# Last even unit of a two-layer cross-attention kernel: V's third block in another gap, and its neighbours in another sequence

## What is computed

```python
def layer(x, ctx, Wq, Wk, Wv, Wo, bias):
    q, k, v = heads(x @ Wq), heads(ctx @ Wk), heads(ctx @ Wv)
    p = softmax(q @ k.T / sqrt(16))
    return merge(p @ v) @ Wo + bias + x
out = layer(layer(x, ctx, *L0), ctx, *L1)
```

## Time and profile before

| what | value |
|---|---|
| device time, median of 3 runs | 936.1 us (931.59, 936.1, 936.99) |
| profiled execution, device time | 934.22 us |
| its span | 932.4 us |
| PE busy | 902.8 us, 97% |
| DVE, ACT, POOL busy | 683.0, 543.1, 399.8 us |

### The profile page before, as it was taken

How to read it: one execution, slowest core, us unless ns; L and a number is a source line. 1 busy time by engine, 2 the same in 40 slices (tenths; PEclk the granted TensorE clock), 3 DMA queues, 4 the chain that set the end, 5 groups by cost and what they waited for, 6 DMA issues and landing times.

```text
span 932.4 us, 28086 instructions
## 1 busy us (share of the span) xinstructions
PE 902.8 (97%) x11518; PEld 682.9 (73%) x11518; DVE 683.0 (73%) x1223; ACT 543.1 (58%) x547; POOL 399.8 (43%) x227
## 2 busy tenths in 40 slices
PE   8899999999999999999999999999999999999897
PEld 5777778777787777777777777777768777777665
DVE  4776786868778686776868788786776878677566
ACT  4456565656656556656656656566655655656552
POOL 3434353624336264366624446363344626432313
PEclk9999999999999999999999999999999999999998
DMA  6313534545444544535555444544534454444442
GB/s 212 91 33 86 141 82 130 140 120 145 103 124 105 164 130 125 143 95 144 142 147 140 103 127 103 135 134 121 148 91 118 123 133 131 111 118 98 96 118 73
DMA packets 80526, 112.41 MB, mean 121 GB/s; under 512 B 21200, under 2 KB 37878, under 8 KB 80400
## 3 DMA queue, kind: packets, MB, share of 16 engines
q1 hardware_dynamic: 80400, 110.61, 44.4%
HBM read 60.24 MB, written 22.24 MB: 88 GB/s over the span
## 4 chain that ended last, share of the span: by engine, by line
PE 71%; SPq 8%; DMA 7%; DVE 6%; issue 3%; ACT 1%; POOL 1%; DVEq 0%; POOLq 0%; ACTq 0%
PE pR L306 23%; PE pR L443 12%; PE pA L390 9%; PE pR L377 7%; PE pR L286 4%; PE pR L328 3%; PE pR L256 3%; SPq L1400 3%; DMA Zg<-Oraw 3%; DMA y<-X 2%; PE pA L396 2%; SPq L1370 2%; PE pR L260 1%; DVE OS L1060 1%; DMA X<-in_xT 1%
## 5 line engine op out<-in xcount | busy, mean ns | idle before, releaser
L753 ACT ACTIVATE P<-pA 77x2048 f32<-77x2048 f32 x160 | 300.3, 1877 | 203.2 <-PE pA L396 203.1
L1004 DVE TENSOR_REDUCE Mx<-pR 128x4 f32<-128x308 f32 (+1 forms) x480 | 259.4, 576 | 31.9 <-PE pR L377 26.6
L1263 POOL TENSOR_TENSOR On<-On,OS 128x1024 f32<-128x1024 f32 (+1 forms) x58 | 105.5, 1841 | 253.2 <-DMA OS<-rd 253.2
L306 PE MATMUL pR<-OS,Wo 128*128 128x512 f32 x638 | 168.2, 403 | 3.0 <-DVE OS L1060 2.3
L443 PE MATMUL pR<-P,VA 77*17 77x256 f32 x2480 | 157.0, 384 | 1.4 <-issue 1.0
L377 PEld LDWEIGHTS pR<-KH,QH 32*128 32x128 f32 x1280 | 96.7, 183 | 76.1 <-issue 49.3
L390 PE MATMUL pA<-QH,KH 32*77 32x256 f32 x1280 | 145.1, 292 | 0.1
L377 PE MATMUL pR<-KH,QH 32*128 32x154 f32 x1280 | 131.7, 283 | 13.3 <-DVE X L1071 3.9
L1228 POOL TENSOR_TENSOR XS<-X,XS 128x1024 fp32r<-128x1024 f32 x31 | 74.0, 2388 | 153.8 <-ACT XS L647 153.8
L306 PEld LDWEIGHTS pR<-OS,Wo 128*128 128x128 f32 x638 | 113.9, 188 | 33.2 <-issue 5.0
L390 PE MATMUL pA<-QL,KH 32*77 32x256 f32 x1280 | 135.0, 275 | 0.0
(11 more groups left out here) (158 smaller groups left out, 1281.9 us busy)
## 6 DMA issues: line engine op xcount, KB each, us to landing
On<-Oraw SPq DMA_DIRECT2D x248, 64.0 KB, 2.6
OS<-rd SPq DMA_DIRECT2D x58, 256.0 KB
C<-in_cT SPq DMA_DIRECT2D x16, 616.0 KB, 7.9
X<-in_xT SPq DMA_DIRECT2D x16, 512.0 KB
y<-X SPq DMA_DIRECT2D x16, 512.0 KB, 4.1
X<-y SPq DMA_DIRECT2D x16, 512.0 KB
out<-X SPq DMA_DIRECT2D x15, 512.0 KB, 4.0
X<-in_xT SPq DMA_DIRECT2D x16, 256.0 KB
```

The costliest lines, as they stand in the source:

```text
L306: f = pe.matmul(p[:, :], W[:, k, c0:c0 + 128], S[:, s, :], start=(i == 0), stop=(i == len(pairs) - 1))
L753: act.activation(P[0:L, i % PR, :, :], pA[0:L, :, :], ACT.Exp, scale=float(D) ** -0.5).then_inc(p_done, 1)
L1004: dve.tensor_reduce(Mx[:, :, :].rearrange("p t (j i) -> p j t i", j=4)[:, j:j + banks, :, i:i + 2], pR[:, bank:bank + banks, 0:2 * LK].rea ...
L1263: pool.tensor_tensor(On[rows, blocks, :], On[rows, blocks, :], recips(u, part).bitcast(F32), ALU.mult).then_inc(o_mul, 1)
```

## The change

On PE, V(15, 2) moves from behind out(28, 0) to between Q(31, 1) and out(28, 1), and from bank 0 to bank 1. ACT takes v_half_copy(15) ahead of S(30, 1) in place of behind it, and V_last(2) behind S(30, 3) in place of behind S(30, 2). DVE takes V(15, 2) right behind Q_lo(31, 1), the two reciprocals of unit 29 behind the maxima (31, 1) in place of ahead of out(28, 1), Q_hi(31, 2) ahead of the maxima (31, 3), and out(28, 2) ahead of Q_lo(31, 2). At the end of unit 29 ACT copies the maxima of unit 30 ahead of O's group 4.

```diff
@@ PE, unit 30
                         Q(u + 1, 1, 2)
+                        V(w - 1, 2, 1)
                         out(z, 1, 0)
                         run(u, 1, n, 2, 0)
                         out(z, 0, 3)
-                        V(w - 1, 2, 0)
                         run(u, 2, n, 2, 0)
@@ ACT, unit 30
                         Q(u + 1, 1)
+                        v_half_copy(w - 1)
                         S(u, 1)
-                        v_half_copy(w - 1)
                         S(u, 2)
-                        V_last(2)
                         q_half_copy(u + 1)
                         o_copy(u, 0)
                         S(u, 3)
+                        V_last(2)
                         split_o(v, 0)
@@ ACT, end of an odd unit
+                    if u == NU - 3:
+
+                        max_rows(n)
+                        o_copy(u, 4)
+                        continue
                     o_copy(u, 4)
                     max_rows(n)
@@ DVE, unit 30
                         split_o(z)
                         Q_lo(u + 1, 1)
+                        V(w - 1, 2)
+                        out(z, 1)
+                        maxima(n, 1, 1, 0, 2)
                         recip_last(v)
                         recip(v)
-                        out(z, 1)
-                        maxima(n, 1, 1, 0, 2)
                         out(z, 0)
-                        V(w - 1, 2)
                         maxima(n, 2, 0, 1, 2)
                         q_sum(u + 1)
+                        Q_hi(u + 1, 2)
                         maxima(n, 3, 0, 1, 2)
-                        Q_hi(u + 1, 2)
+                        out(z, 2)
                         Q_lo(u + 1, 2)
-                        out(z, 2)
                         maxima(n, 4, 1, 0, 2)
```

## The result

The changed kernel takes 936.96 us (median of 20 executions, 934.32 to 940.23), the kernel before 932.79 (20 executions, 929.71 to 936.99). The ratio is 1.0046 with a 95% interval of 1.0035 to 1.0057: some 4.3 us slower, where +0.5 was forecast. The profiled execution took 936.13 with a span of 934.3.

The account below looks back on a forecast made before the run. PE's chain bounds the kernel, judged by PV(30,3)'s end, then SP, a transfer, POOL, ACT and DVE. Terms 0 (Mt) + 0 (V, q_sum) + 0.5 (reciprocals) = +0.5 on 935.2, forecast 935.7 us, range 931.5 to 938.8.

Parts of the forecast that it names:

- Part 1: End of unit 29, ACT: Mt comes 0.1 to 0.2 us earlier, gain ends in o_tail wait; worth 0, bounds -0.2 and +0.1.
- Part 2: PE, unit 30: V's 1.05 us fits the 1.22 gap; 0.24 us gained before run(30,2), 0.7 by Q(31,2).
- Parts 3 and 4: ACT and DVE, unit 30: q_half_copy 1.0 us earlier, at 880.7; PE at step 8 of run(30,4) at 887.0, 2.2 ahead.
- Part 5: Late reciprocals delay SP's spread 1.9 us, then POOL's product and ACT's copy (30,1); step 8 of run(30,4) 0.5 later.
- is absorbed in this wait, 2.7 us long: Inside run(30,4): gains of V's move and earlier q_sum vanish in PE's wait for ACT's copy, adding 0.
- Rival C: SP ahead of spread(29,0): same chain, put_recips issue again 1.27 us and slowest spread; +1.4 us, 936.6; chance 0.15.
- Nothing in that stretch has a second way round: From DVE's copy of O's group (30,3) to the end: the program's end moves exactly as much as PV(30,3).
- The rule that I did weigh: VectorE instruction with two SBUF inputs and GpSimd one reading SBUF exclude each other; Q_lo(31,2) held till about 888.5, forecast unchanged.
- Rival B: Spread on time, run(30,4) passes step 8 at 887.0, gain kept: -1.5 us (2.2 with short Q_lo), 933.7; chance 0.20.

Follow-up runs that it names:

- e6: Kernel before with only V's block moved (PE, ACT's v_half_copy, DVE's sum): 933.98 us, ratio 1.0 to the kernel before.
- e1: Changed kernel with the two reciprocals of unit 29 early again, right behind Q_lo(31,1): 932.59 us, ratio 0.9998 to the kernel before.
- e2: Kernel before with only the two reciprocals moved late, behind the maxima (31,1): 938.09 us, ratio 1.006 to the kernel before.
- e4: Changed kernel with ACT's o_copy(30,1) and S(30,4) ahead of split_o(29,0), reciprocals still late: 933.16 us, ratio 1.0007 to the kernel before.
- e3: Changed kernel with 11 useless matmuls filling PE's wait inside run(30,4), ahead of step 8: 932.77 us, ratio 0.9999 to the kernel before.
- e7: Changed kernel, reciprocals early, O's copy and S(30,4) ahead of split_o(29,0), Q_lo(31,2) behind the maxima (31,4): 931.13 us, ratio 0.9978 to before.
- e9: The same kernel as e7, run again as control: 930.98 us, ratio 0.998 to the kernel before.
- e10: e9 with 4 useless matmuls on PE between V(15,2) and out(28,1): 931.11 us, ratio 0.9977 to the kernel before.
- e8: Kernel before with 3 useless matmuls behind its wait inside run(30,4): 934.49 us, ratio 0.9996 to the kernel before.
- e5: e1 with 4 useless matmuls in PE's wait inside run(30,4): 933.29 us, ratio 0.9993 to the kernel before.

## Why the prediction was wrong, point by point

**Part 1** (Mt ahead of O): the wait for Mt shrank from 0.71 to 0.57 in the profiles and ended in the wait for o_tail, as forecast. No run tested it alone.

**Part 2** (V in the gap): right. The wait ahead of out(28,1) is 0.51 where it was 1.22, run(30,2) waits 0.94 for DVE's read of bank 3 (0.8 forecast), and e6 finds the move worth nothing that can be measured. That interval (1.7 us either way) is too wide to check the 0.24 to 0.7 us forecast. What I took from one row and should not have was the gap: between the profiles with V in it, it is 0.5 to 3.7 us.

**Parts 3 and 4**: right in place. q_half_copy starts at 879.50, on the scale 0.83 earlier than the 881.68 of before (1.0 forecast). PE reached step 8 3.15 before 889.22, at 886.07, where 887.0 less the shift of 1.35 gives 885.65: later than forecast by 0.42.

**Part 5** (the late reciprocals): the mechanism and the order of events are as forecast, step by step. e1 and e2 show that it is the reciprocals, and e4 that it passes over ACT's order; the steps over SP and the transfer between them are read from the profiles alone. First put at 874.71 (876.05 less 1.35), spread at 878.37 (879.65 less 1.35 is 878.30). The transfer took 6.78 to POOL's start where I took 6.0, so step 8 came 1.39 later in place of 0.5. It lay outside the 5.8 to 6.3 that I had allowed (whose upper end gives +0.8, not +0.9).

**The step that failed** is the last one of part 5: "The last exponential and PV(30,4), now at 891.54, follow by the same 0.5, PV(30,3) too, and the end", and with it that the gain of the other parts "is absorbed in this wait, 2.7 us long". I forecast the wait at 2.7 us and priced only its end. The durations behind it were carried over from rows at full clock. But the earlier PE arrives at the wait, the longer it stands idle, and behind the 3.15 us of this wait it ran at half clock: 2.4 us on the profile's path to DVE's copy, 4.2 in the medians (e3). So the gains of V, ACT and q_sum were not absorbed at nothing; they lengthened the wait. Rival C, slower by +1.4, had the same chain and the same gap in it.

A second step failed with it: "Nothing in that stretch has a second way round". With PE at half clock the way over PE itself ended last, if by little, and not the one over SP and the transfer. So not all of the cost has to pass through the copy of O's group (30,3), and the end of the span moved by 3.25 on the scale where the copy moved by 3.82.

The Trainium skill (TensorE: Matmul & The Clock Gate, "HAM oscillation — how this bites in real kernels") describes a loss of this kind: idle gaps on TensorE, there while it waits for a transfer, drop it to 1.2 GHz and the next block starts cold. This case's trace agrees with the level and the sign, 0.50 from 889.22 to 897 behind a wait of 3.15. I held the page's subject for settled because the granted clock was 1.00 almost everywhere, though the mean of the profiled execution of before, 0.997, already said that some microseconds of it were not; they lie in the last unit, behind its wait of 1.46.

**The rule that I did weigh** (SBUF — State Buffer, "Who interferes with whom"): Q_lo(31,2) took 2.49, from 885.29 to 887.78, and POOL's first instruction on the chain ran from 885.15 for 2.36, to 887.51. That is the rule's picture, held and then run, and the row's 1.39 was too low. It bore on the time once the longer wait was gone (e4), and moving Q_lo out of its way was part of the gain in e7; that part was not run by itself.

**Rival B** (the gain kept) was priced at -1.5 at least. e1 shows 0.7 at the same clock: the POOL chain, not the maxima, was the next bound, at 1.10 of waiting. The prediction's own rows had it: ACT's copy (30,1), which frees the bank of step 8, ended at 887.45 + 0.58 = 888.03 in the kernel before, so with a spread on time step 8 could not pass at 887.0, and B was worth 1.1 at most.

**The noise.** I took 935.2, the middle of four executions, for the kernel's time, and the scatter for something without a cause. With 20 executions it is 932.79, so the forecast time of 935.7 stood on a base 2.4 too high. That it came within 1.3 of the 936.96 measured is luck: against the kernel before beside it the change costs 4.2, not 0.5. A part of the scatter goes with the clock, that is with the places where an execution loses it.

**What stays open.** Why the spread of unit 28 takes from 5.8 to 9.1 us from issue to product from one execution to the next; why e7 and e9, the same kernel, had 4 and 1 executions at a low clock; whether e10's fill, and not chance, took the last ones away; and how much of each execution's low clock is lost in unit 30, in the last unit or at the start, since only one execution of each kernel has a profile.

## What to carry to other kernels

When an edit makes the matmul engine reach a wait earlier without ending the wait earlier, do not book the gain as merely absorbed: price the durations behind the wait at half clock as well, and read the granted clock of the stretch behind every long wait. Follow a moved instruction through every in-order list that stands behind it; here two reciprocals of 0.55 us each, taken 3.7 us later, passed over SP, a transfer, POOL and ACT before they stopped PE. And put a copy that frees a bank ahead of an instruction that waits for another engine's long chain.

## What the runs showed of the hardware that I had not expected

- Useless matmuls can make a kernel faster: 11 of 128x512, 2.79 us in a wait, gave 4.2 us. (The kernel before spends 11 such matmuls of its own near its start, at 13.63.)
- The granted clock fell around waits of 3.15 (changed kernel), 2.42 and 1.49 (e2), 3.68 and 1.60 (e6), 3.29 (e7), 2.32 (e8) and 1.46 (before, last unit), and held behind 1.22 (before), 1.29 (e3, ahead of out(28,1)) and 2.07 (e5). The length of the wait alone does not order these. Once down, it stayed at 0.50 from 889.22 to past 897 in the changed kernel and for some 5 us in e7, and 8 matmuls of 128x512 took 3.36 to 3.78 in place of 2.1.
- An execution's mean granted clock goes with its time: in the kernel before, with e1 to e4, 931.74 at 0.998 or more against 934.37 at 0.995 or less. It does not settle it: e3's 12 executions, all at 0.998 or more, still lie from 930.51 to 936.28.
- A DVE subtraction of 128x256 with both inputs in SBUF took 0.42 alone and 1.35 to 2.49 beside a POOL product.
- The same spread of 640 KB of reciprocals let POOL start 5.8 to 9.1 us behind its issue in different executions; in the two slowest (9.05 in e6, 9.01 in e7) PE waited longest ahead of out(28,1), and the clock fell there.
